# Macaron block with a Mamba layer on one Trainium2 core: B and C projected as rows, B three times over, its parts split on rows

## Chip, core and metric

One NeuronCore of a Trainium2 chip runs the whole kernel. The metric is the device time of one execution, in microseconds; the median of the runs shown is 1839.37 us. "Iteration" below is one turn of the kernel's software pipeline, of which a middle one takes about 103 to 106 us.

## What is computed

`x` is 32 sequences of 256 tokens with 128 channels, all float32. Three sublayers follow one another, each on a layer-normalised input and added back:

```python
x = x + 0.5 * ffn(layernorm(x), Wg, W1, W2, W3, Ws1, Ws2, Ws3)
x = x + mamba(layernorm(x), ...)
x = x + 0.5 * ffn(layernorm(x), ...)        # the same weights again
```

`ffn` is a mixture of 8 experts (hidden 176), of which the router weights the two best per token, and a shared expert (hidden 352). `mamba`, cut to what the change touches:

```python
x_in, z = split(x @ W_in + b_in)                 # 256 channels each
xc = silu(causal_conv4(x_in) + conv_b)
Bm, Cm = split(xc @ W_xp + b_xp)                 # 16 states each: the change is here
delta = softplus(xc @ W_dt + b_dt)
h_t = exp(delta_t * A) * h_(t-1) + (delta_t * xc_t) * Bm_t      # per channel and state
y_t = sum_over_states(h_t * Cm_t) + D * xc_t
out = (y * silu(z)) @ W_out + b_out
```

## The kernel before

**Groups and iterations.** Two sequences, 512 tokens (`TG`), make a group, and there are 16 groups. The code is fully unrolled: `body(k)` runs for k = -2 to 17, and in iteration k the scan works on group k, while the first feed-forward layer of group k+2, the projections of group k+1 (steps that `lead(k)` admits) and the second feed-forward layer of group k-1 and k-2 are woven in. In k = 2 to 13 all of them are there.

**Slots.** An iteration has 32 slots. Each of the five engines runs its own in-order program, which goes through the slots in the same order. Which step stands in which slot is a table, `PLAN` (line 54); `UNIT` (line 64) gives the slots of the 14 hidden chunks of each feed-forward pass. A chunk's up-projections are in its slot on TensorE (`ps_h1`, `ps_h2`, lines 1076 and 1098) with the SiLU on ScalarE (line 706); one slot later VectorE multiplies by the routing weight (`GATE`, line 904); two slots later GpSimd multiplies by the SiLU (`JOIN`, line 555, "gated"); four slots later TensorE projects down (`BACK`, line 1090). ScalarE's next SiLUs also need GpSimd's product, since there are four SiLU buffers.

**The scan.** In every even slot 2s, state s is handled: TensorE spreads row s of B over 128 partitions with a selection matrix (`row_b`, line 1058, bf16), VectorE multiplies by `du` (line 876) and runs the scan (line 924, "hist"), ScalarE has made the decays (line 686), GpSimd multiplies by row s of C (line 623, "prod"), and for every pair of states a DMA on GpSimd's queue adds 1 MB to `yacc` (line 640, `accumulate`). The rows of C are broadcast to 128 partitions by way of DRAM: SyncE stores `cT` to `c_rows` (line 392) and loads pairs of rows back (line 397). The routing weights go the same way (`w_rows`, lines 403 and 418), with four buffers.

**B and C before.** Slot 20, `xproj` (line 1150): TensorE makes `xc @ W_xp` with tokens on partitions, in 8 products of 32 columns into `ps_m`, the one PSUM bank that all small steps share in turn (`claim`: a step waits until `misc_taken` counts the reader of the step before). Slot 22, `bparts` (lines 975 and 976): VectorE adds the bias, once as float32 (`bc`) and once as bf16 (the high part of B). Slot 23, `bsplit` (lines 591 to 593): three GpSimd instructions make the middle and low bf16 parts, so that the three add up to float32. Slot 26, `cT`: TensorE transposes C four times, ScalarE copies it to `cT` (line 752). Slot 27, `bT`: TensorE transposes the 96 columns of B's parts four times, ScalarE copies them to `bT` (line 755). `row_b` of the next group's state 0 stands at the end of slot 31 and waits for `bT`. `cT` and the routing weights' `wT` share one buffer, `bounce`, so ScalarE waits at each for the other's store (lines 747 and 751).

**Around it.** On ScalarE slot 20 ends with the decays and `sp_exp` (line 795); then come the SiLUs of slots 21 and 22, `norm1`, `sp_ln`, the SiLU of slot 23 and the copy of the transposed `xn` (line 711), for which TensorE's `logits1` waits (line 1110). `route1` in slot 25 is a chain of small VectorE instructions that ends with "hot" (line 959). `du` (line 969) is VectorE's in slot 28; `weights1` (lines 577 to 584) GpSimd's in slot 28. On SyncE slot 22 holds `store_x`, which stores a finished group, waits until it has landed and loads a new one into the same place (lines 384 and 376) ahead of the routing rows of slots 23 and on.

Of the kernel before, what the change touches and what calls it, by code (L numbers as in the profile page):

```python
# [17 lines left out]
def macaron_kernel(nc, x, W_in, b_in, conv_w, conv_b, W_xp, b_xp, W_dt, b_dt, A_log, D_skip, W_out, b_out,  # L18
# [6 lines left out]
    E, _, H = W1.shape  # L25
# [4 lines left out]
    P = 128  # L30
# [62 lines left out]
    def start(k):  # L93
        return isinstance(k, int) and k < FULL

    def plan(k):
        return START_PLAN if start(k) else PLAN

    def sp_plan(k):
        return START_SP if start(k) else SP_PLAN  # L100

    SETUP_MADE, SETUP_TAPS, SETUP_EDGE = 16, 24, 28

    def first(k):
        return isinstance(k, int) and k == -2

    def enters(k):
        return not isinstance(k, int) or 0 <= k + 2 < G

    def lead(k):  # L110
        return not isinstance(k, int) or 0 <= k + 1 < G

    def scans(k):
        return not isinstance(k, int) or 0 <= k < G

    def tail(k):
        return not isinstance(k, int) or 0 <= k - 1 < G

    def last(k):
        return not isinstance(k, int) or 0 <= k - 2 < G  # L120

    def misc_list(k):
        names = (enters(k) * MISC_ENTRY) + (lead(k) * MISC_LEAD) + (tail(k) * MISC_TAIL)
        return [n for s in range(SLOTS) for n in plan(k).get(s, []) if n in names]

    def before(k, names_of):

        if isinstance(k, int):
            return sum(len(names_of(i)) for i in range(-2, k))
        return sum(len(names_of(i)) for i in range(-2, FULL)) + (k - FULL) * len(names_of(FULL))  # L130

    def turn(k, name):

        return before(k, misc_list) + misc_list(k).index(name) + 1

    def turn_last(k, name):

        after = misc_list(k - 1 if isinstance(k, int) else FULL - 1)
        return before(k, misc_list) - (len(after) - 1 - after.index(name))

    def ffn_no(k, f):

        if isinstance(k, int) and k < FULL:
            return k + 2
        if isinstance(k, int) and k >= G - 2:
            return k + G - 2
        return 2 * k + 1 - f

    def route_no(k, step):

        if isinstance(k, int) and k < 1:
            return k + 2
        if isinstance(k, int) and k >= G - 2:
            return k + G - 1
        return 2 * k + (2 if step.endswith("1") else 1)

    def fcount(k, f, per, n):

        return ffn_no(k, f) * per + n

    def f_parity(k, f):
        return ffn_no(k, f) % 2 if isinstance(k, int) else 1 - f

    def w_turn(k, odd, f, e):

        if isinstance(k, int):
            n = ECHUNK * ffn_no(k, f) + e
            return n % NW, 2 * 16 * (n // NW + 1)
        n = ECHUNK * (2 * odd + 1 - f) + e
        return n % NW, 2 * 16 * (2 * ECHUNK // NW) * (k - odd) + 2 * 16 * (n // NW + 1) + (  # L170
            2 * 16 * (2 * ECHUNK % NW) // NW) * (k - odd)

    def unit(k, odd, slot, lag):
# [4 lines left out]
        if slot - lag + back * SLOTS not in units:  # L178
            return None
# [1017 lines left out]
```

## Time and profile before

| | |
|---|---|
| median of 3 runs | 1839.37 us (1837.52 to 1846.04) |
| the profiled execution's own time | 1839.04 us |
| its span | 1837.3 us |
| TensorE matmul busy | 1658.7 us, 90% |
| VectorE busy | 1478.3 us, 80% |
| GpSimd busy | 1445.7 us, 79% |
| ScalarE busy | 1266.2 us, 69% |
| TensorE clock granted, middle of the run | full (1.00 from 300 to 800 us) |

The span is what the profile covers; the 1.7 us to the own time lie around it. Busy shares are means over fill, middle and drain. Matmuls are pipelined, and so a record's length is not its cost: the distance between the starts of two neighbours is. In a timeline a bracket at a row's end is the idle time ahead of it on that engine and what ended it.

### The profile page before, as it was taken

How to read it: one execution, taken by the hardware profiler on the slowest of the kernel's cores; microseconds unless marked ns; L12 is line 12 of the kernel's file. 1: busy time of each engine (PE TensorE's matmuls, PEld its weight loads, DVE VectorE, ACT ScalarE, POOL GpSimd, SP SyncE). 2: the span in 40 equal slices, each digit the busy share in tenths (PEclk: the TensorE clock that was granted, in tenths of full speed). 3: DMA queues.
4: the chain of work that ended last, by engine and by line, in shares of the span. 5: the costliest groups of instructions: out<-in, count | busy, mean ns of one | idle time of the engine just before them, and what ended most of it. 6: DMA issues, size and time to landing. Idle time of an engine off the chain costs nothing.

```text
span 1837.3 us, 24041 instructions
## 1 busy us (share of the span) xinstructions
PE 1658.7 (90%) x7378; PEld 1001.5 (55%) x7378; DVE 1478.3 (80%) x2241; ACT 1266.2 (69%) x2030; POOL 1445.7 (79%) x1366
## 2 busy tenths in 40 slices
PE   5898788999999999999999999999999999958488
PEld 3454445556555555656555555656555555534255
DVE  1438889989798988989798988989898998989732
ACT  2367678787877778776867777786877777665422
POOL 3336869888898988888888888888898888887753
PEclk9998889999999999999999999999999999969599
DMA  6026768687776868686777867777677868767642
GB/s 158 24 87 141 180 150 193 160 205 173 185 184 162 207 156 201 158 194 170 178 184 170 201 158 189 181 187 184 168 190 172 196 156 192 184 152 186 143 104 69
DMA packets 121287, 304.54 MB, mean 166 GB/s; under 512 B 19299, under 2 KB 40518, under 8 KB 106822
## 3 DMA queue, kind: packets, MB, share of 16 engines
q0 software_dynamic: 18432, 125.84, 34.4%
q1 hardware_dynamic: 98406, 174.46, 33.3%
q10 hardware_dynamic: 4320, 2.71, 0.5%
q8 instruction: 58, 0.95, 0.2%
q14 instruction: 71, 0.58, 0.1%
HBM read 167.67 MB, written 5.24 MB: 94 GB/s over the span
## 4 chain that ended last, share of the span: by engine, by line
POOL 43%; DMA 23%; issue 14%; PE 9%; DVE 7%; ACT 1%; SPq 1%; POOLq 0%; ACTq 0%; DVEq 0%
DMA yacc<-prod 19%; POOL prod L623 18%; POOL gated L555 14%; DVE hist L924 4%; DMA crow<-c_rows 3%; POOL yacc L619 2%; PE ps_y L1090 2%; DVE ps_db L876 2%; POOL yacc L640 1%; PE ps_h1a L1076 1%; SPq L418 1%; PE ps_h2a L1098 1%; PE ps_h1b L1076 1%; PE ps_h2b L1098 1%; POOL xres L610 1%
## 5 line engine op out<-in xcount | busy, mean ns | idle before, releaser
L623 POOL TENSOR_TENSOR prod<-hist,crow 128x1024 f32<-128x1024 f32 x224 | 556.5, 2484 | 204.7 <-DVE hist L924 171.0
L1090 PEld LDWEIGHTS ps_y<-down_w,gated 128*128 128x128 f32 (+1 forms) x3584 | 474.0, 196 | 276.4 <-issue 160.1
L924 DVE TENSOR_TENSOR_SCAN hist<-decay,ps_db 128x1024 f32<-128x1024 f32 x256 | 583.3, 2278 | 2.8
L555 POOL TENSOR_TENSOR gated<-gated,silu 128x512 f32<-128x512 f32 x352 | 493.3, 1450 | 74.4 <-DVE gated L904 71.4
L1090 PE MATMUL ps_y<-down_w,gated 128*128 128x128 f32 (+1 forms) x3584 | 491.8, 282 | 58.0 <-POOL gated L555 56.3
L876 DVE TENSOR_TENSOR ps_db<-du,ps_db 128x1024 f32<-128x1024 f32 x256 | 313.2, 1224 | 114.2 <-PE ps_db L1058 112.1
L686 ACT ACTIVATE decay<-delta,a_neg 128x510 f32<-128x510 f32 x512 | 326.8, 709 | 3.7 <-DVE delta L965 2.2
L706 ACT ACTIVATE silu<-ps_h1a 128x512 f32<-128x512 f32 (+1 forms) x224 | 132.9, 593 | 194.8 <-PE ps_h1a L1076 194.6
L1076 PE MATMUL ps_h1b<-xnT,up_w 128*128 128x512 f32 x448 | 236.7, 610 | 3.6 <-ACT silu L706 3.1
L1098 PE MATMUL ps_h2a<-xnT,up_w 128*128 128x512 f32 (+1 forms) x448 | 236.1, 609 | 1.9 <-DVE gated L904 1.9
L1076 PE MATMUL ps_h1a<-xnT,up_w 128*128 128x512 f32 (+1 forms) x448 | 236.4, 609 | 0.0
L1098 PE MATMUL ps_h2b<-xnT,up_w 128*128 128x512 f32 x448 | 232.0, 600 | 1.4 <-DVE gated L904 1.4
L904 DVE TENSOR_TENSOR gated<-ps_h2b,wrow 128x512 f32<-128x512 f32 x192 | 130.7, 681 | 60.3 <-PE ps_h2b L1098 40.2
L706 ACT ACTIVATE silu<-ps_h1b 128x512 f32<-128x512 f32 x224 | 133.0, 594 | 63.6 <-PE ps_h1b L1076 52.1
L686 ACT ACT_TABLE_LOAD x124 | 159.1, 1283 | 2.2
L904 DVE TENSOR_TENSOR gated<-ps_h2a,wrow 128x512 f32<-128x512 f32 x160 | 107.9, 674 | 46.3 <-PE ps_h2a L1098 36.2
L706 ACT ACT_TABLE_LOAD x111 | 142.4, 1283 | 2.0
L1058 PE MATMUL ps_db<-bT,sel_b 96*128 96x512 bf16 x256 | 102.2, 399 | 41.5 <-DVE hist L924 41.4
L1047 PE MATMUL ps_m<-xnT,w_conv 128*128 128x512 f32 (+3 forms) x256 | 118.2, 596 | 0.0
L1076 PEld LDWEIGHTS ps_h1a<-xnT,up_w 128*128 128x128 f32 (+1 forms) x448 | 85.0, 192 | 56.6 <-issue 47.0
L1076 PEld LDWEIGHTS ps_h1b<-xnT,up_w 128*128 128x128 f32 x448 | 79.1, 194 | 64.0 <-issue 37.5
L640 POOL DMA_DIRECT2D yacc<-prod x112 | 101.6, 908 | 1.6 <-issue 1.3
(136 smaller groups left out, 1937.5 us busy)
## 6 DMA issues: line engine op xcount, KB each, us to landing
yacc<-prod POOLq DMA_DIRECT2D x112, 1024.0 KB, 10.0
crow<-c_rows SPq DMA_DIRECT2D x128, 512.0 KB, 5.0
wrow<-w_rows SPq DMA_DIRECT2D x320, 128.0 KB, 6.3
wrow<-w_rows SPq DMA_DIRECT2D x64, 224.0 KB, 7.0
wrow<-w_rows SPq DMA_DIRECT2D x64, 192.0 KB, 6.4
wrow<-w_rows SPq DMA_DIRECT2D x64, 160.0 KB, 2.9
yacc<-yacc POOLq DMA_DIRECT2D x16, 512.0 KB, 7.8
wrow<-w_rows SPq DMA_DIRECT2D x64, 96.0 KB, 2.9
```

The lines of the kernel that those rows point to most:

```text
L555: nc.gpsimd.tensor_tensor(gated[:, pos % NGATE, :], gated[:, pos % NGATE, :], silu[:, (pos + NCHUNK * f_parity(of, f)) % NSILU, :], ALU.mu ...
L623: nc.gpsimd.tensor_tensor(prod[:, (pair - 1 + odd) % 2, s % 2, :, :], hist[:, s % 2, :, :], c_all, ALU.mult).then_inc(prod_done, 1)
L640: pool.dma_start(yacc[odd][:], prod[:, (pair - 1 + odd) % 2, :, :, :], accum_op=ALU.add).then_inc(acc_done, 16)
L686: ins = nc.scalar.activation(decay[:, s % NA, half, :, 1:LEN], d[:, :, 1:LEN], ACT.Exp, scale=a_neg[:, half, s:s + 1])
L706: nc.scalar.activation(silu[0:r, (pos + NCHUNK * f_parity(k, f)) % NSILU, :], ps_h1[pos % 2][0:r, :], ACT.Silu).then_inc(silu_done, 1)
L876: nc.vector.tensor_tensor(ps_db[:].rearrange("p (h t) -> p h t", h=HALVES), du[par][:], ps_db[:, TG:2 * TG].unsqueeze(1).to_broadcast([P, ...
L904: nc.vector.tensor_tensor(gated[0:r, pos % NGATE, :], ps_h2[pos % 2][0:r, :], factor, ALU.mult).then_inc(h2_taken, 1)
L924: nc.vector.tensor_tensor_scan(hist[:, s % 2, :, :].rearrange("p h t -> p (h t)"), decay[:, s % NA, :, :, :].rearrange("p h b t -> p (h b ...
L1047: nc.tensor.matmul(acc[:, :, late:LEN], w_conv[:, tap, half * P:(half + 1) * P], now[:, :, 0:LEN - late], start=(tap == PAD), stop=False)
L1076: nc.tensor.matmul(ps_h1[pos % 2][0:r, :], up_w[:, 0, j * P:j * P + r], xnT[f][:], start=True, stop=True).then_inc(h1_full, 1)
L1090: ins = nc.tensor.matmul(ps_y[:, t * C:(t + 1) * C], gated[0:rd, posd % NGATE, t * P:(t + 1) * P], down_w[0:rd, jd, :], start=(posd == 0 a ...
L1098: nc.tensor.matmul(ps_h2[pos % 2][0:r, :], up_w[:, 1, j * P:j * P + r], xnT[f][:], start=True, stop=True).then_inc(h2_full, 1)
```

## The change

`W_xp` is laid out as stationary columns, `w_rows_bc`: B's 16 columns at 0, at 32 and at 64, C's at 96 (`BC_ROWS` = 112, the rest zero), and `b_rows_bc` holds the bias in the same way, one per partition. `xproj` becomes two products of 512 columns whose result has B (three times) and C on partitions, tokens along the row. ScalarE writes all 96 rows as bf16 with the bias into `bT` (`b_high`) and C's 16 rows into `cT`, both at the end of slot 20. VectorE forms (value + bias) - high for rows 0 to 63 (`b_rest`, slot 22). ScalarE rounds that to bf16 into `bT[0:64]` (`b_mid`, slot 23). GpSimd subtracts the rounded part on rows 0 to 15, which leaves the low part there (`b_low`, slot 27): the rows from 0 on hold low, from 32 middle, from 64 high. The steps `bparts`, `bsplit`, `cT` and `bT` are gone, with the transposes. `row_b` of a new group's state 0 waits for `b_ready` (GpSimd), SyncE's store of C for `c_made`. `cT` has rows of `bounce` of its own, so the waits between it and `wT` are gone. The constants take six more loads at the start (21 instead of 15).

```diff
-        20: ["sp_exp", "xproj", "scale1"], 21: ["addy1"], 22: ["norm1", "sp_ln", "bparts"], 23: ["xT1", "bsplit"], 24: ["logits1"],
-        25: ["rcopy1", "route1"], 26: ["cT", "delta"], 27: ["bT", "tilt1"], 28: ["weights1", "du"], 30: ["wT1"],
+        20: ["sp_exp", "xproj", "b_high", "scale1"], 21: ["addy1"], 22: ["norm1", "sp_ln", "b_rest"], 23: ["xT1", "b_mid"], 24: ["logits1"],
+        25: ["rcopy1", "route1"], 26: ["delta"], 27: ["b_low", "tilt1"], 28: ["weights1", "du"], 30: ["wT1"],
...
+        w_rows_bc = sb("w_rows_bc", [P, HALVES, BC_ROWS])
+        b_rows_bc = sb("b_rows_bc", [BC_ROWS, 1])
...
-        wT, cT = bounce[0:E, :], bounce
+        wT, cT = bounce[0:E, :], bounce[KP:BC_ROWS, :]
...
-                    sp.wait_ge(misc_taken, turn(g - 1, "cT"))
+                    sp.wait_ge(c_made, g + 1)
...
-                        elif step == "bsplit" and lead(k):
-                            pool.wait_ge(misc_taken, turn(k, "xproj"))
-                            chain = Chain(pool, pool_split, SPLIT_LINKS, k + 1)
-                            hi, md, lo = (bparts[:, :, 32 * q:32 * q + NS] for q in range(PARTS))
-                            chain.link(nc.gpsimd.tensor_tensor(md, bc[:, :, 0:NS], hi, ALU.subtract))
-                            chain.link(nc.gpsimd.tensor_tensor(brem[:], bc[:, :, 0:NS], hi, ALU.subtract))
-                            nc.gpsimd.tensor_tensor(lo, brem[:], md, ALU.subtract).then_inc(bparts_ready, 1)
...
+                        elif step == "b_low":
+                            pool.wait_ge(b_mid_ready, it + 2)
+                            low = bT[nxt][0:NS, :]
+                            nc.gpsimd.tensor_tensor(low, brem[0:NS, :], low, ALU.subtract).then_inc(b_ready, 1)
...
+                        elif step == "b_mid":
+                            act.wait_ge(misc_taken, turn(it, "xproj"))
+                            nc.scalar.activation(bT[nxt][0:64, :], brem[:], ACT.Copy).then_inc(b_mid_ready, 1)
...
+                    for step, it in steps(k, slot):
+                        if step == "b_high":
+                            take(it, "xproj")
+                            nc.scalar.activation(bT[1 - it % 2][:], ps_m[0:KP, :], ACT.Identity, bias=b_rows_bc[0:KP, :]
+                                                 ).then_inc(b_high_ready, 1)
+                            if it >= 0:
+                                act.wait_ge(c_stored, 16 * (it + 1))
+                            nc.scalar.activation(cT, ps_m[KP:BC_ROWS, :], ACT.Identity, bias=b_rows_bc[KP:BC_ROWS, :]
+                                                 ).then_inc(c_made, 1)
...
-                            nc.vector.tensor_tensor(bc[:], rows_in, bias, ALU.add)
-                            nc.vector.tensor_tensor(bparts[:, :, 0:NS], rows_in[:, :, 0:NS], bias[:, :, 0:NS], ALU.add
-                                                    ).then_inc(misc_taken, 1)
...
+                        elif step == "b_rest":
+                            dve.wait_ge(misc_full, turn(it, "xproj"))
+                            dve.wait_ge(b_high_ready, it + 2)
+                            dve.wait_ge(c_made, it + 2)
+                            nc.vector.scalar_tensor_tensor(brem[:], ps_m[0:64, :], b_rows_bc[0:64, :],
+                                                           bT[nxt][0:64, :], ALU.add, ALU.subtract
+                                                           ).then_inc(misc_taken, 1)
...
-                            to_rows(bc[:, :, NS:2 * NS], NS, ident, ps_m).then_inc(misc_full, 1)
...
-                            to_rows(bparts, KP, ident_bf, ps_m[:, 0:TG // 2].bitcast(BF16)).then_inc(misc_full, 1)
...
+                            for half in range(HALVES):
+                                ins = nc.tensor.matmul(ps_m[0:BC_ROWS, :], w_rows_bc[:, half, :], xconv[nxt][:, half, :],
+                                                       start=(half == 0), stop=(half == HALVES - 1))
...
-                        pe.wait_ge(misc_taken, turn(k, "bT"))
+                        pe.wait_ge(b_ready, k + 2)
```

The rest of the diff is another way of writing the counters (tables of steps and passes instead of formulas); it moves no instruction.

GpSimd, slots 22 to 28 of a middle iteration, before. "prod" is a state's product with C, "gated" a chunk's product with its SiLU, `prob` the begin of `weights1`:

```order
L623 TENSOR_TENSOR prod<-hist,crow 128x1024 x2
L632 TENSOR_TENSOR carrier_p<-pow_half,pow_mone 128x1
L640 DMA yacc<-prod 128x2048
L555 TENSOR_TENSOR gated<-gated,silu 128x512
L591 TENSOR_TENSOR bparts<-bc,bparts 128x4x16
L592 TENSOR_TENSOR brem<-bc,bparts 128x64
L593 TENSOR_TENSOR bparts<-brem,bparts 128x4x16
L555 TENSOR_TENSOR gated<-gated,silu 128x512
L623 TENSOR_TENSOR prod<-hist,crow 128x1024
L555 TENSOR_TENSOR gated<-gated,silu 128x512 x2
```

and the same engine and slots in the changed kernel, up to `prob`:

```order
L641 DMA yacc<-prod 128x2048
L559 TENSOR_TENSOR gated<-gated,silu 128x512 x2
L624 TENSOR_TENSOR prod<-hist,crow 128x1024
L559 TENSOR_TENSOR gated<-gated,silu 128x512 x2
L624 TENSOR_TENSOR prod<-hist,crow 128x1024
L633 TENSOR_TENSOR carrier_p<-pow_half,pow_mone 128x1
L641 DMA yacc<-prod 128x2048
L559 TENSOR_TENSOR gated<-gated,silu 128x512
L595 TENSOR_TENSOR bT<-brem,bT 16x512
L559 TENSOR_TENSOR gated<-gated,silu 128x512
L582 TENSOR_TENSOR prob<-tilt,pow_mone 128x8
```

The three small instructions in slot 23, ahead of the product of state 12, are gone; one of 16x512 stands behind the product of state 13 and the gated of slot 27, ahead of that of slot 28.

ScalarE in the changed kernel, slots 20 to 24 (`dtmp` is `sp_exp` and then `sp_ln`):

```order
L795 ACTIVATE dtmp<-dtmp 128x1024
L786 ACTIVATE bT<-ps_m,b_rows_bc 96x512
L790 ACTIVATE bounce<-ps_m,b_rows_bc 16x512
L704 ACT_TABLE_LOAD
L704 ACTIVATE silu<-ps_h1b 128x512
```

```order
L710 ACTIVATE xnT<-ps_m 128x512
L747 ACTIVATE bT<-brem 64x512
L704 ACTIVATE silu<-ps_h1a 128x512
```

Two instructions stand between `sp_exp` and the SiLU of slot 21, and one behind the copy of `xnT`; before, two copies stood in slots 26 and 27 instead, and none here.

## Rows read from the trace of the kernel before

**Rows 1.** The stretches of two middle iterations, by engine (us, then busy us and instructions)
```profile
681.77:785.04 103.27, 99.93 (x462) 60.77 (x462) 91.49 (x140) 79.01 (x128) 89.39 (x85) 1.00 0.76 182
891.37:997.43 106.06, 100.36 (x462) 60.86 (x462) 92.47 (x140) 79.24 (x128) 89.67 (x85) 1.00 0.74 177
```
**Rows 2.** The chain that ended last, by engine, from the page
```profile
POOL 43%; DMA 23%; issue 14%; PE 9%; DVE 7%; ACT 1%; SPq 1%; POOLq 0%; ACTq 0%; DVEq 0%
```
**Rows 3.** Timeline of TensorE, slot 20 on (start us, us, instruction, [idle before])
```profile
688.11 1.87 PE L1150 MATMUL ps_m<-w_xp,xconv 128*128 128x32 f32 x16
689.81 1.10 PE L1076 MATMUL ps_h1b<-xnT,up_w 128*128 128x512 f32 x2
...
701.60 1.06 PE L1110 MATMUL ps_m<-wg,xnT 128*128 128x8 f32 x8 [0.22 <-ACT xnT L711]
...
705.21 0.38 PE L1058 MATMUL ps_db<-bT,sel_b 96*128 96x512 bf16 x1
...
708.04 0.60 PE L1037 MATMUL ps_m<-ident,bc 128*16 128x128 f32 x4
708.47 1.02 PE L1076 MATMUL ps_h1b<-xnT,up_w 128*128 128x512 f32 x2
...
716.21 1.16 PE L1090 MATMUL ps_y<-down_w,gated 128*128 128x128 f32 x8 [1.05 <-POOL gated L555]
...
722.81 1.16 PE L1090 MATMUL ps_y<-down_w,gated 128*128 128x128 f32 x8 [0.45 <-POOL gated L555]
...
728.76 1.16 PE L1090 MATMUL ps_y<-down_w,gated 128*128 128x128 f32 x8 [0.24 <-POOL gated L555]
```
**Rows 4.** Timeline of GpSimd, slots 23 to 28 of the same iteration
```profile
701.48 0.62 POOL L591 TENSOR_TENSOR bparts<-bc,bparts 128x64 bf16<-128x64 f32 x1
702.17 0.31 POOL L592 TENSOR_TENSOR brem<-bc,bparts 128x64 f32<-128x64 f32 x1
...
702.82 1.27 POOL L555 TENSOR_TENSOR gated<-gated,silu 128x512 f32<-128x512 f32 x1
704.04 2.36 POOL L623 TENSOR_TENSOR prod<-hist,crow 128x1024 f32<-128x1024 f32 x1
...
710.49 3.26 POOL L623 TENSOR_TENSOR prod<-hist,crow 128x1024 f32<-128x1024 f32 x1 [1.63 <-DVE hist L924]
...
714.57 2.82 POOL L555 TENSOR_TENSOR gated<-gated,silu 128x512 f32<-128x512 f32 x2
```
**Rows 5.** Timeline of VectorE, slots 25 to 28 of the same iteration
```profile
704.68 1.80 DVE L959 TENSOR_TENSOR hot<-lanes,topi 128x64 f32<-128x64 f32 x1
706.41 1.22 DVE L876 TENSOR_TENSOR ps_db<-du,ps_db 128x1024 f32<-128x1024 f32 x1
...
716.85 1.63 DVE L969 TENSOR_TENSOR du<-delta,xconv 128x1024 f32<-128x1024 f32 x1
```
**Rows 6.** Timeline of ScalarE, slots 20 to 24 of the same iteration
```profile
691.82 1.04 ACT L795 ACTIVATE dtmp<-dtmp 128x1024 f32<-128x1024 f32 x1
...
700.95 0.59 ACT L711 ACTIVATE xnT<-ps_m 128x512 f32<-128x512 f32 x1
```
**Rows 7.** Groups of instructions by line and form (count, busy us, mean ns, idle before)
```profile
L767 ACT ACTIVATE zs<-ps_m,b_in_c 128x512 f32<-128x512 f32 x32 | 21.8, 680 | 17.3 <-PE ps_m L1134 17.3
L911 DVE SCALAR_TENSOR_TENSOR xres<-ps_y,xres 128x512 f32<-128x512 f32 x32 | 21.9, 685 | 19.8 <-PE ps_y L1090 19.8
```
**Rows 8.** Timeline of SyncE, slots 22 and 23 of the iteration at 891 us
```profile
902.16 0.41 SPq L384 DMA_DIRECT2D out<-xres  x1
...
909.20 1.43 SPq L418 DMA_DIRECT2D wrow<-w_rows  x2
```
**Rows 9.** Timeline of VectorE, waits for a routing row in slot 26: first, third, last of five
```profile
501.15 0.69 DVE L904 TENSOR_TENSOR gated<-ps_h2b,wrow 128x512 f32<-128x512 f32 x1 [1.33 <-DMA wrow<-w_rows]
...
919.93 0.69 DVE L904 TENSOR_TENSOR gated<-ps_h2b,wrow 128x512 f32<-128x512 f32 x1 [2.59 <-DMA wrow<-w_rows]
...
1439.41 0.69 DVE L904 TENSOR_TENSOR gated<-ps_h2b,wrow 128x512 f32<-128x512 f32 x1 [1.37 <-DMA wrow<-w_rows]
```

More of the change, by code:

```diff
@@ L91, in macaron_kernel @@
     }
[L93 to L100, printed above, removed]
     SETUP_MADE, SETUP_TAPS, SETUP_EDGE = 16, 24, 28
-    def first(k):
-        return isinstance(k, int) and k == -2
+    PLANS = {k: START_PLAN for k in range(-2, FULL)}
+    UNITS = {k: START_UNIT for k in range(-2, FULL)}
+    SP_PLANS = {k: START_SP for k in range(-2, FULL)}
     def enters(k):
-        return not isinstance(k, int) or 0 <= k + 2 < G
+        return 0 <= k + 2 < G
@@ L126, in before @@
[L126 to L171, printed above, removed]
@@ L173, in unit @@
-    def unit(k, odd, slot, lag):
-        back = slot < lag
-        of, parity = (k - 1, 1 - odd) if back else (k, odd)
-        units = START_UNIT if start(of) else UNIT
-        if slot - lag + back * SLOTS not in units:
-            return None
-        f, pos = units[slot - lag + back * SLOTS]
-        return (of, parity, f, pos) if (last(of) if f else enters(of)) else None
-    def home(engine, group):
-        return group % XS if isinstance(group, int) else engine.snap(group % XS)
-    def iterations(engine, body):
+        return 0 <= k - 2 < G
@@ new lines, in macaron_kernel @@
+    ROLES = [(enters, ["stats0", "scale0", "norm0", "xT0", "logits0", "rcopy0", "route0", "tilt0", "weights0", "wT0"]),
+             (lead, ["addy0", "stats2", "scale2", "norm2", "xT2", "in0a", "in0", "in1a", "in1", "in2", "in3", "dt0", "dt1",
+                     "sp_exp", "sp_ln", "xproj", "b_high", "b_rest", "b_mid", "b_low", "delta", "du"]),
+             (tail, ["fold", "gate_y0", "gate_y1", "outproj", "resid", "stats3", "scale3", "ln_norm", "ln_scale",
+                     "ln_shift", "ln_add", "stats1", "scale1", "norm1", "xT1", "logits1", "rcopy1", "route1", "tilt1",
+                     "weights1", "wT1"]),
+             (last, ["addy1"])]
@@ new lines, in macaron_kernel @@
+    ALL = [(name, it) for k in range(-2, G + 2) for slot in range(SLOTS) for name, it in steps(k, slot)]
+    MISC = {step: n + 1 for n, step in enumerate(s for s in ALL if s[0] in MISC_NAMES)}
+    ROUTES = [(it, name[4]) for name, it in ALL if name in ("tilt0", "tilt1")]
+    STAT_STEPS = [s for s in ALL if s[0] in ("stats0", "stats1", "stats2", "stats3")]
+    UNIT_AT = {}
+    for k in range(-2, G + 2):
+        for slot, (f, pos, *shift) in UNITS.get(k, UNIT).items():
+            it = k + sum(shift)
+            if (last(it) if f else enters(it)):
+                UNIT_AT[(k + 2) * SLOTS + slot] = (it, f, pos)
@@ L189, in iterations, with unit, home @@
+    def unit(k, slot, lag):
+        return UNIT_AT.get((k + 2) * SLOTS + slot - lag)
+    def home(group):
+        return group % XS
+    def iterations(body):
         for k in range(-2, G + 2):
@@ L707, in body @@
+                        nc.scalar.activation(silu[0:r, (pos + NCHUNK * f_parity(of, f)) % NSILU, :],
                                              ps_h1[pos % 2][0:r, :], ACT.Silu).then_inc(silu_done, 1)
-                    for step in plan(k).get(slot, []):
-                        if step == "xT0" and enters(k) or step == "xT1" and tail(k) or step == "xT2" and lead(k):
-                            take(k, step)
+                    for step, it in steps(k, slot):
+                        nxt, entering, ahead, behind = 1 - it % 2, home(it + 2), home(it + 1), home(it - 1)
+                        if step == "xT0" or step == "xT1" or step == "xT2":
+                            take(it, step)
```

500 lines of the change are left out of this document (246 added, 254 removed).

## Prediction

> **What bounds the kernel now.** First the stretches of two middle iterations [rows 1]: TensorE is recorded busy for 99.93 of 103.27 us, GpSimd for 89.39, VectorE for 91.49. So TensorE looks like the bound, and whatever is taken off it should count. Then the chain that ended last [rows 2]: 43% of it is GpSimd, 23% DMA and only 9% TensorE. The two don't exclude each other: the timeline of TensorE tells where it is held up. It runs without a gap nearly everywhere, but in every middle iteration it waits at the same places for GpSimd's "gated": 1.05 us at 716.21, 0.45 at 722.81, 0.24 at 728.76 [rows 3]. These are the down-projections that belong to GpSimd's products of slots 27, 29 and 31. In between, GpSimd is never idle: its last gap before them is 1.63 us ahead of the product of state 13 [rows 4], which waits for VectorE's scan, and from 710.49 on it works without a break past the last of TensorE's three waits. So the end of an iteration is set like this: VectorE's scan of state 13 in slot 26 starts a stretch in which GpSimd is the late one (slots 26 to 31), TensorE takes over that lateness at 728.76, and from there on TensorE is the bound until slot 26 of the next iteration.
>
> What lets the scan of state 13 begin is of two kinds. In 7 of the 12 full iterations it is VectorE's own row of work: "hot" at 704.68 took 1.80 us, until 706.48, since it got going only when GpSimd's product of state 12 was through (704.04 and 2.36, so 706.40) [rows 4, 5]. In the other 5 the multiplication just ahead of the scan waits for a routing row, from 1.33 to 2.59 us [rows 9]. That row was issued at 909.20, behind the store of the finished group (902.16, [rows 8]), which itself follows TensorE's last down-projection of slot 20; nothing that is done in slots 21 to 26 moves it.
>
> **The change part by part.**
>
> *TensorE.* `xproj` costs 1.70 us now (688.11 to 689.81 [rows 3]). In its place come two products of 512 columns, of which one is recorded with 1.02 us (708.47), so at most 2.04; I take no difference. C's four transposes go: 0.43 us (708.04 to 708.47 [rows 3]). B's four in bf16 are not longer: between 0 and 0.43, and I take 0.22 as the middle. Together 0.65 us less in slots 26 and 27. TensorE stands still for 1.05 us right behind them, for GpSimd [rows 3], so I count nothing; where that cover was gone it would be 0.65 for each of 16 groups.
>
> *GpSimd, slot 23.* Three small instructions go, 1.34 us (701.48 to 702.82 [rows 4]). Behind them are 1.63 us of waiting for the scan of state 13, so by themselves they give nothing. By way of "hot" they may: the product of state 12 could be through up to 1.2 us earlier, and "hot" with it. See ScalarE for what is late next.
>
> *GpSimd, slot 27.* `b_low` is new, 16 partitions by 512 columns. No such row exists. One end: a product over 128 partitions and 512 columns takes 1.27 us (702.82), or 1.41 as the mean of two with VectorE in the way (2.82 for two at 714.57). The other end: 128x64, which has the same number of elements, takes 0.31 (702.17) [rows 4]. I take 1.25, since all groups of GpSimd rows here that differ in columns differ in time, and partitions are what the engine works on side by side. It stands behind gated of slot 27 and ahead of that of slot 28, in the stretch without a gap, so it delays the gated of slots 28 to 31 by all of it, and TensorE's waits at 722.81 and 728.76 grow: 1.25 us for an iteration. What it waits for, `b_mid`, is four slots back.
>
> The Trainium skill (GPSIMD Engine Reference, "Instruction dispatch") says that each of the eight cores works on its own 16 partitions of an instruction, and that the instruction is complete only when all eight have answered. By that rule 16 partitions are as long as 128, and the sum stays; by the count of elements `b_low` would be 0.31, and the sum becomes that of the first rival. No row of this trace decides it.
>
> *ScalarE.* `b_high` and the write of `cT` are with bias out of PSUM; the like takes 0.68 us [rows 7], records of neighbours overlap a little: 1.0 to 1.36, I take 1.2. They stand behind `sp_exp` (691.82). From there to the copy of `xnT` (700.95 [rows 6]) ScalarE has no idle time, and `logits1` on TensorE already waits for that copy (0.22 us at 701.60 [rows 3]). So `logits1` comes 1.2 us later, and with it the row of B for state 13, from 705.21 to 706.4. VectorE's multiplication by `du` needs it, about 0.4 us after its start, at 706.8 instead of 706.41 [rows 5]. So what GpSimd gives by way of "hot" is taken by this, and 0.4 us more: 0.4 in the 7 iterations of the first kind, nothing in the 5 that wait for the routing row. `b_mid` (0.59 like the copy [rows 6]) stands behind `xnT`; it delays the SiLU of slot 24, which is needed two slots later. The two copies of slots 26 and 27 go, in a place where ScalarE waits for TensorE: nothing.
>
> *VectorE.* `b_rest` costs 0.685, as the same instruction with a PSUM operand does [rows 7]; two short ones go, so between nothing and 0.685 is added, in slot 22, ahead of the row of B that already comes late. I count nothing of it beside ScalarE's delay, which covers it. Its new waits (`b_high`, `c_made`) end near 694 (691.82, 1.04 and the 1.2 above), two slots before it.
>
> *SyncE, start and end.* The six more small loads stand among constants whose first reader is in slot 24 of the first iteration: nothing. C is stored earlier, but from the same place of SyncE's queue: nothing. In iterations 0 and 1 GpSimd is busy through slot 23 as well, so the 1.34 us removed pay for the 1.25 added; -1 and 14 have hardly any gated to delay. I count 0 for these four, with 1.3 us each either way in the bounds.
>
> **Sum.** 5 x 1.25 + 7 x (1.25 + 0.4) = 6.3 + 11.6 = 17.9 us on the profiled execution's 1839.0, so **1857 us**, 1.0% more. The profiled execution is 0.3 us under the median of the runs, so the same number holds for the median. The runs before spread over 8.5 us, so 0.5% (9.2 us) is about what can be told from no change.
>
> **Rivals.**
>
> *`b_low` is short.* If it goes by elements, 0.31 us: 5 x 0.31 + 7 x 0.71 = 6.5, 1845.5 us. For it: the small instruction. Against: everything else on this engine.
>
> *The gain by way of "hot" arrives.* If ScalarE's two instructions don't reach `logits1` (they overlap more, or the SiLU of slot 21 isn't late), the scan of state 13 begins up to 1.1 us earlier in 7 iterations: 5 x 1.25 + 7 x 0.15 = 7.3, 1846.3 us. Against: the 0.22 us that `logits1` already waits. With both of these rivals together: 5 x 0.31 - 7 x 0.79 = -4.0, 1835 us. For these three together 20 in 100.
>
> *TensorE is the bound after all, and the kernel is faster.* The 90% busy share speaks for it. If the lateness of GpSimd in slots 27 to 31 is taken up elsewhere, since TensorE's three waits shrink by themselves once its own work in slots 26 and 27 is shorter, the 0.65 us count for 16 groups: 10.4 us, and 13.8 with B's transposes at 0.43: 1825 to 1829 us. It decides only if `b_low` delays TensorE by less than about 0.1 us; 0.24 us of wait at 728.76 speak against. 12 in 100.
>
> *The routing rows shift.* Each iteration of the second kind is up to 2.8 us longer than one of the first (106.06 against 103.27 [rows 1]). If the new timing makes more or fewer of them, that is some 5 us to either side of my forecast; it belongs to its range.
>
> The Trainium skill (Advanced Engine Details and Errata, "GPSIMD Details") has GpSimd and VectorE in conflict where a VectorE instruction has two SBUF inputs. `b_rest` has one of its two in PSUM, so by this rule it is not held up; were it, a product of 2.36 us on GpSimd would stand before it.
>
> **How the numbers follow.** Forecast 68 in 100, the two middle rivals 20, the fast one 12. By the first, 1857 with 1849 to 1866: `b_low` at 1.0 to 1.41, ScalarE at 0 to 0.6, the ends at plus or minus 2.6, the routing rows at 5. The range that should hold 8 in 10 takes in the second group: 1835 to 1866. Slower by over 0.5% (above 1848.6) 0.68, within 0.20, faster 0.12.
>
> **What would show it.** In the changed profile: `b_low` at about 1.25 us in slot 27, with no gap on GpSimd from the product of state 13 to past slot 31; TensorE's wait at slot 31's down-projection grown from 0.45 to over 1 us; `logits1` waiting over 1 us for `xnT`; middle iterations of 105 us instead of 103.3. If `b_low` is under 0.5 us, or the sum of TensorE's waits for gated is not larger than 1.7 us in an iteration, the forecast is wrong by that step; if `logits1` waits as before, by the other.

## The result, and the profile after

| | before | changed |
|---|---|---|
| median (range), 7 runs each | 1841.49 us (1837.52 to 1846.04) | 1851.88 us (1850.31 to 1854.77) |
| ratio, 95% interval | | 1.0065 [1.005, 1.008] |
| the profiled execution's own time, its span | 1839.04, 1837.3 us | 1853.38, 1851.6 us |

Slower by 10.4 us by the medians, by 12 by the ratio (which is that of the record and not the quotient of these two medians), by 14.3 by the profiled executions. An iteration is counted here from the end of TensorE's wait ahead of the second group of `w_dt` products to the same point of the next one. Two middle iterations of the changed kernel, columns as in [rows 1]:

```profile
687.67:792.87 105.20, 99.73 (x442) 58.99 (x442) 91.60 (x139) 79.92 (x129) 89.49 (x83) 1.00 0.75 179
898.54:1003.26 104.72, 99.74 (x442) 58.98 (x442) 92.18 (x139) 79.83 (x129) 89.59 (x83) 1.00 0.75 179
```

Eleven middle iterations take 1157.3 us (372.04 to 1529.36) where they took 1146.1 (370.83 to 1516.91): 11.2 of the 14.3 us lie there, 1.02 for each. Another 1.2 lie ahead of them and 1.8 behind. TensorE has 20 records fewer in an iteration and is busy as long as before, give or take 0.2 to 0.6 us; what grew is its waiting. Its timeline, rows that begin with a wait:

```profile
702.00 1.13 PE L1068 MATMUL ps_h1b<-xnT,up_w 128*128 128x512 f32 x2 [0.67 <-ACT silu L704]
...
708.93 1.06 PE L1103 MATMUL ps_m<-wg,xnT 128*128 128x8 f32 x8 [0.79 <-ACT xnT L710]
...
715.69 1.13 PE L1068 MATMUL ps_h1b<-xnT,up_w 128*128 128x512 f32 x2 [0.16 <-ACT silu L704]
...
723.27 1.16 PE L1082 MATMUL ps_y<-down_w,gated 128*128 128x128 f32 x8 [1.01 <-POOL gated L559]
...
730.66 1.16 PE L1082 MATMUL ps_y<-down_w,gated 128*128 128x128 f32 x8 [1.24 <-POOL gated L559]
...
736.59 1.16 PE L1082 MATMUL ps_y<-down_w,gated 128*128 128x128 f32 x8 [0.23 <-POOL gated L559]
```

Against [rows 3], two waits for ScalarE are new or longer (0.67 for a SiLU, and 0.79 where `logits1` waited 0.22), and the wait at slot 31's down-projection is 1.24 instead of 0.45. `logits1` starts 21.26 us into the iteration (708.93 - 687.67), before 19.83: 1.43 later. The wait behind that one did not grow (0.23, before 0.24): TensorE, held back once, comes to it late as well. The cause of the first two is in ScalarE's timeline, and that of the last in GpSimd's:

```profile
697.72 1.04 ACT L795 ACTIVATE dtmp<-dtmp 128x1024 f32<-128x1024 f32 x1
698.67 0.66 ACT L786 ACTIVATE bT<-ps_m,b_rows_bc 96x512 bf16<-96x512 f32 x1
699.36 0.68 ACT L790 ACTIVATE bounce<-ps_m,b_rows_bc 16x512 f32<-16x512 f32 x1
700.05 1.28 ACT L704 ACT_TABLE_LOAD   x1
701.35 0.60 ACT L704 ACTIVATE silu<-ps_h1b 128x512 f32<-128x512 f32 x1
```
```profile
709.66 2.35 POOL L624 TENSOR_TENSOR prod<-hist,crow 128x1024 f32<-128x1024 f32 x1 [0.78 <-DVE hist L916]
...
717.57 3.25 POOL L624 TENSOR_TENSOR prod<-hist,crow 128x1024 f32<-128x1024 f32 x1 [3.08 <-DVE hist L916]
...
721.63 1.58 POOL L559 TENSOR_TENSOR gated<-gated,silu 128x512 f32<-128x512 f32 x1
722.87 1.15 POOL L595 TENSOR_TENSOR bT<-brem,bT 16x512 bf16<-16x512 f32 x1
723.98 1.25 POOL L559 TENSOR_TENSOR gated<-gated,silu 128x512 f32<-128x512 f32 x1
```

`b_high` and `cT` stand ahead of the SiLU that TensorE waits for. `b_low` took 1.15 us, between two gated products and with no gap, while GpSimd had stood idle for 3.08 us just before (1.63 in [rows 4]). And one thing got smaller: VectorE's waits for routing rows. Groups of instructions between 300 and 1600 us, first of the kernel before, then of the changed one (count, busy us, mean ns, idle before):

```profile
L904 DVE TENSOR_TENSOR gated<-ps_h2b,wrow 128x512 f32<-128x512 f32 x150 | 101.9, 679 | 9.2 <-DMA wrow<-w_rows 9.2
L904 DVE TENSOR_TENSOR gated<-ps_h2a,wrow 128x512 f32<-128x512 f32 x125 | 84.1, 673 | 6.8 <-DMA wrow<-w_rows 6.8
```
```profile
L896 DVE TENSOR_TENSOR gated<-ps_h2b,wrow 128x512 f32<-128x512 f32 x149 | 101.3, 680 | 5.0 <-DMA wrow<-w_rows 4.4 <-PE ps_y L1082 0.5
L896 DVE TENSOR_TENSOR gated<-ps_h2a,wrow 128x512 f32<-128x512 f32 x124 | 83.3, 672 | 2.4 <-DMA wrow<-w_rows 1.8 <-PE ps_h2b L1090 0.5
```

They fell from 16.0 us to 6.2. So there are three things to test: what `b_low` costs in its place, what ScalarE's two instructions cost in theirs, and whether the waits for rows paid a part of both.

### The profile page after: what moved, and what is told of

Read it like the earlier page. It is cut to its first block, busy times and chain, and to the rows that moved or that the text cites. A ratio compares the mean times of both kernels' runs of the same rounds, so it can differ in the third digit from the quotient of the medians.

```text
span 1851.6 us, 23360 instructions
## 1 busy us (share of the span) xinstructions
PE 1649.3 (89%) x7058; PEld 971.5 (52%) x7058; DVE 1488.6 (80%) x2226; ACT 1278.3 (69%) x2046; POOL 1442.5 (78%) x1334
## 4 chain that ended last, share of the span: by engine, by line
POOL 38%; PE 18%; issue 16%; DMA 15%; ACT 7%; DVE 6%; POOLq 0%; ACTq 0%; SPq 0%; DVEq 0%
POOL prod L624 15%; DMA yacc<-prod 14%; POOL gated L559 13%; PE ps_y L1082 4%; DVE hist L916 3%; POOL yacc L620 3%; PE ps_h1a L1068 2%; PE ps_h2b L1090 2%; PE ps_h1b L1068 2%; PE ps_h2a L1090 2%; PE ps_m L1040 1%; DVE ps_db L871 1%; ACT decay L687 1%; ACT silu L704 1%; ACT L704 1%
```

## The experiments

Ratios are to the kernel before on the same chip; the medians come from several chips. "Iteration" is the mean of eleven middle ones in the profile. The letters A, B and C in the text are the theories that each expectation sets against one another.

| run | kernel | median us | ratio, 95% interval | iteration us |
|---|---|---|---|---|
| | changed | 1851.88 | 1.0065 [1.005, 1.008] | 105.21 |
| e1 | `b_low` in slot 26 | 1843.34 | 1.0009 [0.9999, 1.0019] | 104.42 |
| e2 | C evacuated by VectorE | 1850.48 | 1.0052 [1.0038, 1.0066] | 104.97 |
| e3 | e1 and e2 | 1839.49 | 0.9997 [0.9983, 1.0011] | 104.30 |
| e4 | changed, 8 transposes more | 1849.15 | 1.005 [1.0037, 1.0062] | 105.24 |
| e5 | before, SyncE's edit | 1829.35 | 0.9944 [0.9924, 0.9963] | 103.27 |
| e6 | changed, SyncE's edit | 1845.39 | 1.0031 [1.0019, 1.0042] | 104.70 |
| e7 | e1, SyncE's edit | 1834.55 | 0.9977 [0.9965, 0.9988] | 103.89 |
| e8 | e3, SyncE's edit | 1826.67 | 0.9931 [0.9913, 0.9948] | 103.03 |
| e9 | e8, 8 transposes more | 1825.4 | 0.9917 [0.99, 0.9933] | 103.05 |
| e10 | e5, one GpSimd operation more | 1838.24 | 1.0 [0.9988, 1.0013] | 103.94 |
| e11 | e6, one GpSimd operation more | 1869.47 | 1.0159 [1.0142, 1.0176] | 106.24 |
| e12 | e8, `b_high` by VectorE | 1823.85 | 0.9904 [0.9882, 0.9926] | 102.81 |

### First look: each cost taken out, and the saving put back (e1 to e4)

e1, `b_low` one slot earlier:
```diff
-        25: ["rcopy1", "route1"], 26: ["delta"], 27: ["b_low", "tilt1"], 28: ["weights1", "du"], 30: ["wT1"],
+        25: ["rcopy1", "route1"], 26: ["b_low", "delta"], 27: ["tilt1"], 28: ["weights1", "du"], 30: ["wT1"],
```


> Base: the changed kernel, 1851.9 us. b_low moves from slot 27 to slot 26, ahead of the product of state 13, where GpSimd stands idle 3.08 us in the iteration that starts at 687.67. Theory A (b_low costs what it takes, because nothing hides it in slots 27 to 31): 1.15 us an iteration come back in 11 to 12 iterations, 13 to 14 us, so 1838 to 1839 us; the idle time before the down-projections of slots 29 and 31 falls from 1.01 and 1.24 us to under 0.6 each. Theory B (the length of an iteration is set by when the routing rows land, and what is saved is waited for them): at most half of it comes back, 1845 to 1849 us, and the sum of VectorE's waits for wrow rises from 6.3 us to over 12.

8.5 us came back by the medians and 10.3 by the ratios, of the 13 to 14 that A gave; B allowed for half, to 1845. The iterations are shorter by 0.79 us, and the waits before the down-projections of slots 29 and 31 fell to 0.48 and 0.46, as A says. The waits for rows stayed where they were (7.3 us), so B's reason is not seen.

e2, C's rows from ScalarE's slot 20 to VectorE's slot 22, behind `b_rest`:
```diff
-                            nc.scalar.activation(cT, ps_m[KP:BC_ROWS, :], ACT.Identity, bias=b_rows_bc[KP:BC_ROWS, :]
-                                                 ).then_inc(c_made, 1)
+                            nc.vector.tensor_scalar(cT, ps_m[KP:BC_ROWS, :], b_rows_bc[KP:BC_ROWS, :], None, ALU.add
+                                                    ).then_inc(misc_taken, 1)
```


> Base: the changed kernel, 1851.9 us. The evacuation of C leaves ScalarE's queue in slot 20 and stands on VectorE behind b_rest in slot 22, ahead of 1.57 us in which VectorE waits anyway. Theory A (ScalarE's two new evacuations delay the silu, xnT and logits1, each by as much as they take): the idle time before logits1 falls from 0.79 to about 0.2 us, the scan of state 13 comes 0.5 to 0.65 us earlier, and 12 iterations give back 6 to 8 us: 1844 to 1846 us. Theory B (b_low alone makes the loss, ScalarE's part is hidden behind the waits for routing rows): within 2 us of 1851.9.

Neither as it stood. `logits1` waits 0.27 us, as A says; but the time fell by 1.4 us only (2.4 by the ratios). What A gave is in another column: VectorE waits 17.9 us for routing rows, where the changed kernel has 6.2.

e3, both edits:

> Both edits at once. Theory A: the two savings add up, 19 to 22 us, 1830 to 1833 us, which is below the kernel before (1841.5). Theory B (routing rows or the next resource take over): no better than 1840 us. With the two costs gone, TensorE's saving of 0.65 us an iteration (8 transposes fewer) may be seen for the first time: the iteration would be 102.6 to 103.3 us.

B: the savings did not add up. The median is 1839.5, and 14.8 us of waits for rows are there. Its iterations are of two kinds again:
```profile
684.55:787.61 103.06, 99.89 (x441) 58.90 (x442) 92.30 (x140) 79.04 (x128) 89.91 (x83) 1.00 0.74 182
787.61:892.66 105.05, 100.07 (x441) 58.81 (x442) 92.54 (x140) 79.13 (x128) 89.86 (x83) 1.00 0.74 179
```

e4, eight transposes of constants on TensorE, in the shapes and slots (`pe_f` in 26, `pe_b` in 27) of those removed:
```diff
+                        elif step in ("pe_f", "pe_b"):
+                            pe.wait_ge(misc_taken, sum(n[0] in MISC_NAMES for n in ALL[:ALL.index((step, it))]))
+                            if step == "pe_f":
+                                to_rows(ident[:, 0:NS].unsqueeze(1).to_broadcast([P, TILES, NS]), NS, ident, ps_m)
+                            else:
+                                to_rows(ident_bf[:, 0:KP].unsqueeze(1).to_broadcast([P, TILES, KP]), KP, ident_bf,
+                                        ps_m[:, 0:TG // 2].bitcast(BF16))
```


> The changed kernel with eight more transposes on TensorE, in the two slots (26 and 27) and of the two shapes that it removed (0.43 and 0.22 us), of constants, into the free bank of PSUM. Theory A, on which the prediction counted TensorE's saving at nothing: they lie ahead of down-projections that wait 1.01 and 1.24 us for gated, so the time stays within 2 us of 1851.9. Theory C (TensorE's saving is felt in full, and the loss elsewhere was larger by as much): 0.65 us in 12 iterations, 1859 to 1860 us.

A. 105.24 us an iteration against 105.21, and the time is not above that of the changed kernel (2.7 us under it, a little more than the 2 that A gave): TensorE's saving is worth nothing here.

### The waits for routing rows taken out (e5 to e8)

In slot 22 SyncE waits until the store of x has landed (902.16 to 908.76 in the kernel before), reloads, and only then issues the routing rows [rows 8]. The edit moves that wait and the load to the end of slot 29 (printed as it stands in e6; in e5 it is the same with `k` for `it`):
```diff
-        28: ["w0:9", "next_c0"], 29: ["w0:10"], 31: ["store_w1", "w1:0", "w1:1", "w1:2", "w1:3"],
+        28: ["w0:9", "next_c0"], 29: ["w0:10", "load_x"], 31: ["store_w1", "w1:0", "w1:1", "w1:2", "w1:3"],
...
-                sp.wait_ge(x_stored, 16 * (g + 1))
...
+                        elif step == "load_x":
+                            sp.wait_ge(x_stored, 16 * (it - 1))
+                            if it - 2 + XS < G:
+                                load(it - 2 + XS, home(it - 2), row_of(it - 2 + XS))
```


> The kernel before, with one edit of SyncE's order: it no longer waits in slot 22 for the store of x to land (about 6 us) before it goes on to the routing rows of slots 23 and 24; that wait and the load behind it stand at the end of slot 29. Theory A (VectorE's 16.1 us of waits for routing rows in the middle of the kernel before come from rows issued late behind that wait): they fall to under 6 us and the time by 7 to 12 us, to 1829 to 1834 us, with all middle iterations near 103.3 us. Theory B (the rows are late because they land slowly, 5.5 to 6 us, wherever they are issued): within 2 us of 1840.5.

> The same edit on the changed kernel. Theory A (the change lost less than the 1.65 us an iteration that its first kind of iteration pays, because VectorE came later to the routing rows and waited 9.8 us less for them): here only 6.3 us of such waits are left to save, so the time falls by 1 to 5 us, to 1846 to 1850 us, and the changed kernel then stands 15 to 19 us over the kernel before with the same edit, where it stood 10.4 over it without. Theory B (the waits for rows have nothing to do with the size of the loss): the distance of the two stays 9 to 12 us.

> b_low in slot 26 and SyncE's edit together, ScalarE's two evacuations as in the changed kernel. Theory A: 1.15 us an iteration less than the changed kernel with SyncE's edit, 1834 to 1838 us. Theory B: no better than b_low in slot 26 alone, 1842 to 1844 us.

> All three edits: b_low in slot 26, C evacuated on VectorE, SyncE's edit. Theory A (the 14.8 us of waits for routing rows that came back when the two costs were taken out are what held that kernel at 1839.5): 1829 to 1833 us, below the kernel before by 0.4 to 0.6%, and level with the kernel before with SyncE's edit or below it. Theory B (another bound at about 103.3 us an iteration): 1836 us or more. If TensorE's 0.65 us an iteration counts at last, the middle iterations come out under 103.0 us.

A in all four by its reason, not by every number: e6 lies 0.6 us and e8 2.3 us below A's range, and `b_low` gave 0.81 us an iteration in e7 instead of 1.15. SyncE issues the routing rows 2.2 us behind the store now, where it was 7.0 in [rows 8]:
```profile
688.17 0.41 SPq L384 DMA_DIRECT2D out<-xres  x1
690.38 1.49 SPq L417 DMA_DIRECT2D wrow<-w_rows  x2
```
Not one wait for a row is left in the middle of e5, e6 and e8, and one of 0.2 us in e7. The first group shows it for e5 between 300 and 1600 us, and its iterations are now of one length:
```profile
L904 DVE TENSOR_TENSOR gated<-ps_h2b,wrow 128x512 f32<-128x512 f32 x151 | 102.6, 679 | 0.0
```
```profile
677.38:780.65 103.27, 99.94 (x461) 60.76 (x462) 92.28 (x140) 79.00 (x128) 89.44 (x85) 1.00 0.73 182
1297.12:1400.38 103.26, 99.92 (x461) 60.75 (x462) 92.27 (x140) 79.01 (x128) 89.55 (x85) 1.00 0.75 182
```
So are those of the changed kernel with the edit (e6), of that with `b_low` in slot 26 (e7), and of that with C on VectorE as well (e8):
```profile
686.33:791.03 104.70, 99.75 (x442) 58.98 (x442) 92.17 (x139) 79.87 (x129) 89.47 (x83) 1.00 0.74 179
```
```profile
682.88:786.77 103.89, 99.73 (x442) 58.98 (x442) 91.36 (x139) 79.84 (x129) 89.79 (x83) 1.00 0.76 181
```
```profile
680.55:783.59 103.04, 99.89 (x442) 58.90 (x442) 92.23 (x140) 79.05 (x128) 89.79 (x83) 1.00 0.75 182
```
With nothing of chance in an iteration each part has its price, taken out in this order: the change 1.43 us (104.70 - 103.27), `b_low` in slot 27 0.81 of it (104.70 - 103.89), `cT` on ScalarE 0.86 (103.89 - 103.03), and all the rest of the change together gains 0.24 (103.03 against 103.27). And the part of the waits: by the medians changed and before stand 10.4 us apart (12 by the ratios), with SyncE's edit 16.0. The changed kernel lost less than it cost, since it comes later to rows that are late anyway: 16.0 us of waits before, 6.2 after. What the waits hide is ScalarE's part. With them `cT` on ScalarE costs only 0.24 us an iteration (105.21 against e2's 104.97) or 0.12 (e1's 104.42 against e3's 104.30), without them 0.86; `b_low` in slot 27 costs 0.79 (105.21 - 104.42) or 0.67 (104.97 - 104.30) with them and 0.81 without.

### GpSimd's and TensorE's prices again, without that disturbance (e9 to e12)

e9 is e8 with e4's transposes.

> Base: the kernel with all three edits (e8, 1826.7 us, middle iterations of 103.03 us in its profile), with the eight transposes of constants of e4 on TensorE again in slots 26 and 27. Theory A (GpSimd's and VectorE's chain sets the iteration here too; the down-projections behind the transposes wait 0.48 and 0.46 us for gated): the middle iterations grow by at most 0.1 us, the time stays within 2 us. Theory C (with the other costs gone TensorE's saving is felt): 0.5 to 0.65 us an iteration, 103.5 to 103.7 us, 1833 to 1835 us in all.

A: 103.05 us an iteration. The timeline of TensorE shows the transposes taken up by the waits around them: 0.24 us at slot 29's down-projection where e8 has 0.48, and e8's 0.16 for a SiLU shortly before it is gone:
```profile
708.66 0.60 PE L1029 MATMUL ps_m<-ident 128*16 128x128 f32 x4
711.71 0.39 PE L1029 MATMUL ps_m<-ident_bf 128*96 128x128 bf16 x4
716.03 1.16 PE L1081 MATMUL ps_y<-down_w,gated 128*128 128x128 f32 x8 [0.24 <-POOL gated L559]
```

e10 puts one operation on GpSimd in slot 27 of the kernel before, and e11 one in the changed kernel, ahead of `b_low` (`same` is `brem`, `none` are columns of `w_rows_bc` that hold zero):
```diff
+                            nc.gpsimd.tensor_tensor(spare[:], w_in[0:NS, :], w_in[0:NS, :], ALU.subtract)
```
```diff
+                            nc.gpsimd.tensor_tensor(same, same, none, ALU.add).then_inc(brem_kept, 1)
+                            pool.wait_ge(brem_kept, it + 2)
```


> Base: the kernel before with SyncE's edit (e5, 1829.4 us, middle iterations of 103.27 us). One operation more on GpSimd in slot 27, of b_low's size (16x512) and on constants, its result unused; all else as before. Theory A (what stands in GpSimd's queue in slot 27 delays gated and the product of state 14, whatever partitions it has): it takes 1.1 to 1.25 us, and the iterations grow by 0.8 to 1.2 us, to 104.1 to 104.5 us, 1839 to 1844 us. Theory B (an operation on 16 of 128 partitions is short, 0.3 us, or is hidden): under 103.7 us, under 1835 us.

> Base: the changed kernel with SyncE's edit (e6, 1845.4 us, middle iterations of 104.70 us). One operation more on GpSimd ahead of b_low in slot 27: brem plus zeros, 64x512 float32, in place, and b_low waits for it. Theory A (cost by elements along a partition, not by partitions): this operation takes 1.1 to 1.3 us, as b_low's 1.15 us on 16 partitions, and the iterations grow by 0.8 to 1.3 us, to 105.5 to 106.0 us, 1855 to 1861 us. Theory B (64 partitions cost more than 16): it takes over 2 us. Theory C (b_low's own 0.8 us an iteration comes from somewhere else than its place in the queue): no growth.

e10 lies just under A's lower edge, 0.67 us more an iteration and 8.9 in all, and well over B: the operation took 1.03 us on 16 partitions. e11 is a miss: the added operation took 1.57 on 64 partitions, between A's 1.3 us and B's 2, the iteration grew by 1.54, and the median of 1869.5 is 8.5 us above A's range. Its rows say why; first GpSimd's, then VectorE's of the same time:
```profile
729.11 1.57 POOL L597 TENSOR_TENSOR brem<-brem,w_rows_bc 64x512 f32<-64x512 f32 x1
730.76 2.02 POOL L599 TENSOR_TENSOR bT<-brem,bT 16x512 bf16<-16x512 f32 x1
732.75 1.25 POOL L559 TENSOR_TENSOR gated<-gated,silu 128x512 f32<-128x512 f32 x1
733.97 0.19 POOL L582 TENSOR_TENSOR prob<-tilt,pow_mone 128x8 f32<-128x8 f32 x1
```
```profile
729.51 2.26 DVE L966 TENSOR_TENSOR du<-delta,xconv 128x1024 f32<-128x1024 f32 x1
```
`du` has both inputs in SBUF. It started at 729.51, while GpSimd's addition ran to 730.68, and ended at 731.77, 1.09 later. `b_low` started at 730.76 and ended at 732.78, 1.01 behind `du`. So each waits for the other to be through. In e6, the changed kernel with SyncE's edit, it is much the same (GpSimd, then VectorE), but `du` waits for two instructions of GpSimd that follow each other without a gap:
```profile
719.77 1.58 POOL L559 TENSOR_TENSOR gated<-gated,silu 128x512 f32<-128x512 f32 x1
721.00 1.15 POOL L595 TENSOR_TENSOR bT<-brem,bT 16x512 bf16<-16x512 f32 x1
722.12 1.26 POOL L559 TENSOR_TENSOR gated<-gated,silu 128x512 f32<-128x512 f32 x1
723.35 1.17 POOL L582 TENSOR_TENSOR prob<-tilt,pow_mone 128x8 f32<-128x8 f32 x1
```
```profile
721.41 3.05 DVE L962 TENSOR_TENSOR du<-delta,xconv 128x1024 f32<-128x1024 f32 x1
```
GpSimd's gated ends at 723.38, `du` at 724.46, `prob` at 724.52. In e7, without `b_low` there, the three end at 719.11, 720.20 and 720.24:
```profile
716.33 2.78 POOL L559 TENSOR_TENSOR gated<-gated,silu 128x512 f32<-128x512 f32 x2
718.79 1.45 POOL L582 TENSOR_TENSOR prob<-tilt,pow_mone 128x8 f32<-128x8 f32 x1
```
```profile
717.96 2.24 DVE L962 TENSOR_TENSOR du<-delta,xconv 128x1024 f32<-128x1024 f32 x1
```
GpSimd's stretch from the first gated to the end of the second is 3.61 us with `b_low` and 2.78 without, and these 0.83 are passed on through `du` to `prob`, to the product of state 14 and to the gated behind it: the 0.81 of the iteration.

Why 0.8 us and not the 1.15 of `b_low`'s record? The records of neighbours on GpSimd overlap, and what counts here is how far the ends lie apart. The gated ahead of `b_low` ends at 721.35 and `b_low` at 722.15, 0.80 later. It is the same in e10:
```profile
715.90 1.58 POOL L556 TENSOR_TENSOR gated<-gated,silu 128x512 f32<-128x512 f32 x1
717.13 1.03 POOL L589 TENSOR_TENSOR spare<-w_in 16x512 bf16<-16x512 f32 x1
```
The ends are 717.48 and 718.16, 0.68 apart, and the iteration grew by 0.67. That the ends count is a reading of two cases and was not tested by a run of its own.

e12, `b_high` from ScalarE's slot 20 to VectorE's slot 21:
```diff
-                            nc.scalar.activation(bT[1 - it % 2][:], ps_m[0:KP, :], ACT.Identity, bias=b_rows_bc[0:KP, :]
+                            nc.vector.tensor_scalar(bT[nxt][:], ps_m[0:KP, :], b_rows_bc[0:KP, :], None, ALU.add
```


> Base: the kernel with all three edits (e8, 1826.7 us, middle iterations of 103.03 us). The writing of B's high parts goes from ScalarE's slot 20 to VectorE's slot 21, ahead of the addition of y, so that ScalarE has nothing of B and C left before xnT. In e8 the copy xnT still comes 0.57 us later in the iteration than in the kernel before. Theory A (that 0.57 us is b_high, and VectorE's short time at hot can be had in full once it goes): logits1 and the scan of state 12 come 0.3 to 0.57 us earlier, the iterations are 102.5 to 102.8 us, 1820 to 1824 us in all. Theory B (VectorE, 92.2 of 103 us busy in an iteration, has no room for 0.75 us more there): its scans come later instead, 103.0 to 103.8 us, 1826 to 1836 us.

The time is A's, the iteration (102.81) at the edge of it: 0.22 us came, not 0.57. `xnT` did come 0.57 us earlier, but `xT1` on TensorE now waits 0.58 us for C's rows on VectorE, where e8 has 0.17:
```profile
696.53 0.63 PE L1029 MATMUL ps_m<-ident,xn 128*128 128x128 f32 x4 [0.58 <-DVE bounce L968]
```
That this wait took the rest is argued and not tested. This is the fastest kernel of the study by its median, 0.96% under the kernel before, though its interval and e9's overlap. SyncE's edit alone (e5) has 0.56 of that, so the change with its steps in better places is worth about 0.4%.

## Why the prediction was right, and where its terms were off

It said 1857 with a range from 1835 to 1866, slower with 0.68; the median is 1851.9. The direction and the two costs that make it are shown by the runs; the size is in part luck, since `b_low` was put too high and ScalarE's part too low. By its steps:

- *TensorE's saving counts nothing.* Right, and shown twice (e4, e9). The rival by which TensorE is the bound falls, although TensorE is busy for 97% of an iteration.
- *`b_low` takes 1.25 us and delays the gated behind it by all of it.* 1.15 us on record, and the place was the reason (e1, e7). What failed is "by all of it": 0.81 us an iteration, since its end lies only 0.80 behind that of the gated ahead of it. The prediction saw `hot` held up by GpSimd, but did not ask the same of `du` (1.63 us in [rows 5]). `du`, and `prob` behind it, tie the two engines together at just this place. Of the two waits of TensorE that were to grow, one did (0.45 to 1.24). The rival of a short `b_low` falls.
- *ScalarE's two instructions bring `logits1` 1.2 us later.* 1.43. The sign named for it, `logits1` waiting over 1 us, did not show in that form: TensorE waits 0.67 us at a SiLU before it and 0.79 at `logits1`. Of the delay 0.4 was to reach the scan of state 13; it was 0.64 (into the iteration 26.38 in e5, 27.02 in e6), and `cT` alone costs 0.86 an iteration. This term of the sum was mis-sized low.
- *GpSimd's 1.34 us of slot 23 give nothing, since the gain by way of `hot` is taken by ScalarE.* Right in the changed kernel: `hot` took 0.64 instead of 1.80, and VectorE then waited 0.86 for the row of B.
```profile
711.46 0.64 DVE L952 TENSOR_TENSOR hot<-lanes,topi 128x64 f32<-128x64 f32 x1
712.96 1.23 DVE L871 TENSOR_TENSOR ps_db<-du,ps_db 128x1024 f32<-128x1024 f32 x1 [0.86 <-PE ps_db L1051]
```
  In e8 this gain arrives: the scan of state 12 starts 0.52 us later than in e5 (19.29 against 18.77), that of state 13 0.22 earlier (26.16 against 26.38).
- *5 iterations of one kind and 7 of the other, the routing rows some 5 us to either side.* The iterations did not keep their kinds. Of the eleven middle ones five were longer than an undisturbed one before, by 1.4 to 3.1 us; after the change it is eight, by 0.3 to 1.2 us. A delay ahead of the routing row is paid out of the wait for it, which shrank by 9.8 us in all. For a middle iteration the prediction's mean is 1.47 us (1.65 in six, 1.25 in five), and 1.02 was measured. About half of the gap is this step: the waits gave back 0.41 us an iteration (1.43 - 1.02) where the prediction had 0.18 (0.4 in five of eleven). The other half is sizes: 1.43 for the undisturbed kind where the sum had 1.65, too much for `b_low`, too little for ScalarE.
- *Start and end count nothing.* Up to the first middle iteration 1.2 us were lost, within the 1.3 allowed for each. But that is 2.1 us won and 3.3 lost: the one iteration at the end of the start takes 3 us longer. It does so in every kernel with rows of B and C (100.24 against 96.89 us before, 100.09 in e6 against 97.25 in e5), and e12, without ScalarE's part, still has 99.66. The profile shows a difference in the granted clock, which the runs did not follow up; first before, then changed:
```profile
273.94:370.83 96.89, 89.13 (x401) 53.89 (x402) 89.31 (x134) 77.99 (x124) 86.72 (x82) 0.98 0.73 178
```
```profile
271.80:372.04 100.24, 90.27 (x382) 53.78 (x382) 90.75 (x133) 78.84 (x125) 86.45 (x80) 0.95 0.73 172
```
  The clock is the third number from the right: 0.98 in the three kernels that make B and C as before (before, e5, e10), and 0.95 to 0.97 in the eleven others. Whether this is the cause or comes of longer waits is open.

e5's profiled execution (1825.0) is 4 us under its median, so the distances of single profiles are less sure than the lengths of iterations.

## What to carry to other kernels

Where one engine is late and another "busy for 97%", a new instruction costs by its place in the late engine's queue, not by its length: the same `b_low` cost 0.81 us an iteration more in slot 27 than in slot 26, where it stands in a wait of 2.6 to 3.1 us (in e7 1.46 us of it are left). Before two versions are compared, take out the waits that move about by themselves; here one blocking wait in SyncE's queue hid a quarter to a third of the change's cost, most of it ScalarE's part, and with it gone each part could be priced to 0.1 us. A step moved off the fast engine lands somewhere: see that it doesn't stand ahead of what the bound engine waits for.

## What the runs showed of the hardware

In these traces VectorE's instructions with two inputs in SBUF and GpSimd's do not get done beside each other: the second waits for the end of the first, and in e6 for that of the one behind it too (`du` starts at 721.41 beside `b_low`, the gated follows without a gap and ends at 723.38, and `du` at 724.46). `hot` ends within 0.1 us of the end of GpSimd's product before the change (706.48 and 706.40 in [rows 4, 5]) and after (712.10 and 712.01); `du` ends 1.08 to 1.09 us behind GpSimd's instruction in e6, e7 and e11. The Trainium skill (SBUF — State Buffer, "Who interferes with whom") has such a rule: a VectorE instruction with two SBUF inputs contends with a GpSimd instruction that reads SBUF, the shared port pair is an exclusive lock, and the order of issue decides who blocks. By that rule, the trace agrees; the records don't show it as idle time but as longer instructions.

GpSimd's time goes mainly by the elements along a partition: 1.15 us for 16x512 where 128x512 takes 1.25 to 1.58, and 1.57 for 64x512, against 0.31 for 128x64 [rows 4]. The rule that the prediction named (GPSIMD Engine Reference of the Trainium skill, "Instruction dispatch") is borne out in the main. By their starts a gated and `b_low` take 1.23 and 1.12 us in e6 (719.77, 721.00, 722.12). By the ends 16x512 comes out shorter, 0.68 to 0.80 us; whether fewer partitions or the bf16 result make that was not tested.

ScalarE's way out of PSUM with a bias took 0.67 and 0.68 us (96x512 and 16x512); the two without a bias that the change removed took 0.59 each in the trace of the kernel before.
